# Second layer's experts from the fourth chunk on: down products as three products of halves, gate applied to each expert's sum

## The reference, cut to what matters

```python
logits = x @ router_w + router_b                      # 9 columns: 8 experts and one "null"
...                                                   # probs = softmax(logits); top 2 kept as gates
h = jax.nn.gelu(jnp.einsum('btd,edf->ebtf', x, w1), approximate=False)   # e = 8, f = 512
y = jnp.einsum('ebtf,efd->ebtd', h, w2)
out = jnp.einsum('bte,ebtd->btd', gates[..., :E], y) + gates[..., E:] * x
...
x = x + gb * out
```

## Time and profile before

| | |
|---|---|
| time, median of 3 runs | 1898.88 us |
| span of the profiled execution | 1901.1 us |
| TensorE busy | 1669.5 us, 88% of the span |
| VectorE busy | 1393.2 us, 73% |
| ScalarE busy | 790.3 us, 42% |
| GpSimd busy | 680.6 us, 36% |
| the chain that ended last, by engine | PE 34%, DVE 13%, POOL 11%, issue 10% |
| its largest line | PE psum L1428 (`down1`) 10% |
| mean granted clock of TensorE | 0.953 of full speed |
| `down1`, line 1428 | 512 records, 261.9 us busy, mean 597 ns |

### The profile page before, as it was taken

The page is one execution under the profiler, slowest core; times in us unless marked ns, Lnnn a source line. Parts: engine busy times, 40 slices in busy tenths (PEclk is TensorE's granted clock), DMA queues, the critical chain, the costliest instruction groups (busy, mean ns, idle before and its releaser), DMA issues.

```text
span 1901.1 us, 25452 instructions
## 1 busy us (share of the span) xinstructions
PE 1669.5 (88%) x7212; PEld 1043.8 (55%) x7212; DVE 1393.2 (73%) x2638; ACT 790.3 (42%) x1486; POOL 680.6 (36%) x610
## 2 busy tenths in 40 slices
PE   2789889851899999999999999999998999999999
PEld 1455555441665656656556565565665555555555
DVE  5787777558676696896987979979789678544444
ACT  1476766721433324334234253352433643433333
POOL 2011111100000492781945918639378077000000
PEclk9998989955899999999999999999999999999999
DMA  7544444010667777665666667667564111111110
GB/s 272 163 124 121 114 117 131 22 64 0 196 226 228 208 259 202 193 203 178 205 185 184 197 183 195 204 187 211 172 190 127 40 45 53 42 51 55 50 49 29
DMA packets 167960, 269.60 MB, mean 142 GB/s; under 512 B 23220, under 2 KB 61453, under 8 KB 164661
## 3 DMA queue, kind: packets, MB, share of 16 engines
q1 hardware_dynamic: 164227, 266.40, 47.5%
q10 hardware_dynamic: 1586, 1.30, 0.2%
q0 software_dynamic: 2048, 0.79, 0.2%
HBM read 233.78 MB, written 34.62 MB: 141 GB/s over the span
## 4 chain that ended last, share of the span: by engine, by line
PE 34%; DVE 13%; POOL 11%; issue 10%; DMA 3%; ACT 2%; SPq 1%; DVEq 0%; POOLq 0%; ACTq 0%
PE psum L1428 10%; POOL e_prod L1798 7%; PE psum L1321 6%; PE psum L1323 5%; PE psum L1322 5%; PE psum L1330 4%; DVE psum L1729 3%; POOL e_phi L1798 3%; DMA rw<-rw_fm 2%; DVE e_hm L1732 2%; DVE e_y L1610 2%; DVE e_vbar L1610 2%; DVE e_state L1684 1%; PE psum L1367 1%; DMA e_ring<-w_split 1%
## 5 line engine op out<-in xcount | busy, mean ns | idle before, releaser
L1553 ACT ACTIVATE e_gu<-psum 128x512 f32<-128x512 f32 (+1 forms) x368 | 219.2, 598 | 597.7 <-DVE e_hm L1732 302.4
L1321 PE MATMUL psum<-e_hhi,e_ring 128*128 128x512 f32 x704 | 432.7, 615 | 27.2 <-DMA e_ring<-w_split 9.4
L1330 PE MATMUL psum<-e_hm,w_d 128*128 128x512 f32 (+1 forms) x736 | 382.3, 601 | 15.0 <-DVE e_hm L1735 6.5
L1798 POOL TENSOR_TENSOR e_prod<-e_state,e_phi 128x512 f32<-128x512 f32 x256 | 353.8, 1420 | 2.4 <-POOL e_phi L1798 1.7
L1729 DVE TENSOR_TENSOR psum<-psum,rw 128x512 f32<-128x512 f32 x352 | 243.9, 693 | 119.7 <-PE psum L1323 87.9
L1766 DVE TENSOR_TENSOR e_hm<-psum,rw 128x512 f32<-128x512 f32 x256 | 174.6, 689 | 174.7 <-ACT psum L1578 173.6
L1322 PE MATMUL psum<-e_hhi,e_ring 128*128 128x512 f32 x704 | 279.9, 398 | 0.0
L1323 PE MATMUL psum<-e_hlo,e_ring 128*128 128x512 f32 x704 | 279.8, 397 | 0.0
L1732 DVE TENSOR_TENSOR e_hm<-psum,e_gu 128x512 f32<-128x512 f32 x352 | 243.6, 692 | 36.4 <-ACT e_gu L1553 12.5
L1428 PE MATMUL psum<-e_hm,w_gu 128*128 128x512 f32 x512 | 261.9, 597 | 6.6 <-DVE w_d L1747 5.5
L1578 ACT ACTIVATE psum<-psum 128x512 f32<-128x512 f32 x256 | 148.8, 582 | 251.6 <-PE psum L1323 233.9
(11 more groups left out here) (226 smaller groups left out, 2189.2 us busy)
## 6 DMA issues: line engine op xcount, KB each, us to landing
e_ring<-w_split SPq DMA_DIRECT2D x308, 256.0 KB, 4.0
rw<-rw_fm SPq DMA_DIRECT2D x192, 176.0 KB
qk_parts<-at_part SPq DMA_DIRECT2D x96, 192.0 KB, 2.9
rw<-gates_fm SPq DMA_DIRECT2D x72, 256.0 KB, 3.2
w_split<-e_ring SPq DMA_DIRECT2D x44, 256.0 KB, 3.2
rw<-rw_fm SPq DMA_DIRECT2D x64, 160.0 KB
at_qs<-qk_parts SPq DMA_DIRECT2D x16, 576.0 KB
at_ks<-qk_parts SPq DMA_DIRECT2D x16, 576.0 KB
```

Source lines behind the costliest of these rows:

```text
L1321: pe.matmul(out, w_hi, x_hi, start=first, stop=False)
L1330: mm = pe.matmul(ps[:, ACC, :], weights_at(T, WD + P * j, P)[0:rows(j), :], hm[0:rows(j), slot(j), :], start=(j == 0), stop=(j == HT - 1))
L1553: a(act_g[0:r, j % 2, :], ps[0:r, GB[j % 2], :], ACT.Silu).then_inc(silu_done, 1)
L1798: ins = tt(out[:, at], x[:, at], y[:, at], op)
```

## The change

The weights w2 are split too. In chunk 1, ScalarE rounds each of the 32 tiles of w2 (128x128) into the room that the first layer's down weights left (`w2_high`), and VectorE subtracts to get the low halves (`w2_low_half`, in the ring and in `sel_buf`). From chunk 3 (`HALVED`) on, Gelu goes straight from PSUM into the ring `hm`, ungated. ScalarE copies it to its high half (`gelu_high`), one tile behind the Gelu; VectorE subtracts to get its low half (`gelu_low`). `down1_halves` makes three products of halves in place of one float32 product, and sums only over the four tiles of an expert, in banks `YB` by turns. VectorE then multiplies the expert's sum by the gate and adds it to `null` (`add_expert`), at tile j = 4e + 6 for expert e, and for the last expert at tile 2 of the next chunk, followed by `add_result`, the two multiply-adds on x. `null` is now made at j = 4, and the gates' buffers come free with the expert's sum. Besides, the setup's semaphore `eps_set` is merged into `pool_done`. The core of the diff:

```diff
+            def down1_halves(c, j, k):
+                e, g = j // F1T, nth(c, j)
+                if k == HALVED:
+                    pe.wait_ge(w1l_done, T1 + j + 1)
+                    ...
+                if j % F1T == 0 and (k > HALVED or e >= 2):
+                    pe.wait_ge(gated, NE1 * (c - HALVED) + e - 1)
+                pe.wait_ge(glo_done, g + 1)
+                three(ps[:, YB[e % 2], :], part(w2_high(j)), w2_low_half(j), gelu_parts[:, 0, j % RING1, :],
+                      gelu_parts[:, 1, j % RING1, :], j % F1T == 0, j % F1T == F1T - 1).then_inc(ydown_done, 1)
...
+            def gelu_high(c, j, k):
+                ...
+                if k > HALVED or j >= RING1:
+                    act.wait_ge(ydown_done, nth(c, j) - RING1 + 1)
+                act.wait_ge(gelu_done, T1 * c + j + 1)
+                a(gelu_parts[:, 0, j % RING1, :], hm[:, j % RING1, :], ACT.Copy).then_inc(ghi_done, 1)
...
             def block1(c, k):                    # ScalarE
                 for j in range(T1):
                     g = T1 * c + j
+                    if j == 0 and k > HALVED:
+                        gelu_high(c - 1, T1 - 1, HALVED + 1)
                     if j == 0 and k > 0:
                         act.wait_ge(up1_done, g)
                         act.wait_ge(h1_kept, c + 1)
                         h_high(0, c)
                     act.wait_ge(up1_done, g + 1)
...
+                        a(hm[:, j % RING1, :], ps[:, HB[j % 2], :], ACT.Gelu).then_inc(gelu_done, 1)
+                        if j > 0:
+                            gelu_high(c, j - 1, k)
...
+                    if k == 1:
+                        if j == 0:
+                            act.wait_ge(acc_done, CHUNKS)
+                        a(part(w2_high(j)), weights_at(T, w2_low(j), P), ACT.Copy).then_inc(w1h_done, 1)
...
+            def add_expert(c, e, k):             # VectorE
+                n = NE1 * (c - HALVED) + e
+                dve.wait_ge(ydown_done, F1T * (n + 1))
+                dve.wait_ge(r1_in[e % RB_SLOTS], 16 * (NE1 // RB_SLOTS) * c + 16 * (e // RB_SLOTS + 1))
+                v.tensor_tensor(xc[:], ps[:, YB[e % 2], :], rb[:, e % RB_SLOTS, :], ALU.mult).then_inc(gated, 1)
+                dve.wait_ge(gated, n + 1)
+                v.tensor_tensor(null, null, xc[:], ALU.add).then_inc(acc1_read, 1)
...
+            def gelu_low(c, j):
+                dve.wait_ge(ghi_done, nth(c, j) + 1)
+                v.tensor_tensor(gelu_parts[:, 1, j % RING1, :], hm[:, j % RING1, :], gelu_parts[:, 0, j % RING1, :].bitcast(F32),
+                                ALU.subtract).then_inc(glo_done, 1)
...
+                    if k == 1:
+                        if j == 0:
+                            dve.wait_ge(ur_done, HT * CHUNKS)
+                        dve.wait_ge(w1h_done, T1 + j + 1)
+                        v.tensor_tensor(w2_low_half(j), weights_at(T, w2_low(j), P), part(w2_high(j)).bitcast(F32), ALU.subtract)\
+                            .then_inc(w1l_done, 1)
...
+                    if j % F1T == 2 and (k > HALVED or k == HALVED and j > F1T):
+                        e = j // F1T - 1
+                        ...
+                        add_expert(c if e >= 0 else c - 1, e % NE1, k)
+                        if e < 0:
+                            add_result(c - 1)
```

More of the change, by code:

```diff
@@ L1063, with w2_high @@
 NULL_AT = WD + P * (2 * T1 - 2 * FREE_G)
+HALVED = 3
+def w2_high(j):
+    return WD + P * j
 def experts(nc, T, A, out):
@@ L1173, in experts @@
         down1_done = sem("down1_done")
+        ghi_done = sem("ghi_done")
+        glo_done = sem("glo_done")
+        ydown_done = sem("ydown_done")
+        gated = sem("gated")
         acc1_read = sem("acc1_read")
@@ L1250, in part, with w2_low_half, nth @@
             return weights_at(T, at, P, "_r")
+        def w2_low_half(j):
+            return ring[:, P * j:P * (j + 1)] if j < T1 // 2 else T["sel_buf_r"][:, P * (j - T1 // 2):P * (j - T1 // 2 + 1)]
+        def nth(c, j):
+            return T1 * (c - HALVED) + j
         @block.sync
@@ L1455, in block1 @@
                         pass
+                    elif j >= LAG1 and k >= HALVED:
+                        down1_halves(c, j - LAG1, k)
                     elif j >= LAG1:
                         down1(c, j - LAG1, k)
+                    elif k > HALVED:
+                        down1_halves(c - 1, T1 - LAG1 + j, HALVED + 1)
                     elif k > 0:
@@ L1464, in _ @@
             for j in range(T1 - LAG1, T1):
-                down1(CHUNKS - 1, j, 1)
+                down1_halves(CHUNKS - 1, j, HALVED + 1)
         @block.scalar
@@ new lines, in add_result, with gate_tile @@
+            def add_result(c):
+                dve.wait_ge(acc1_read, HALVED + NE1 * (c - HALVED + 1))
+                for i in range(CB):
+                    b = CB * c + i
+                    x = cols(x_fm, b, SEQ)
+                    ins = v.scalar_tensor_tensor(x, null[:, i * SEQ:(i + 1) * SEQ], T["gate"][:, 3, ds(b, 1)], x, ALU.mult, ALU.add)
+                ins.then_inc(x_done, 1)
+            def gate_tile(c, j, k):
+                e, g = j // F1T, T1 * c + j
+                dve.wait_ge(gelu_done, g + 1)
+                if j % F1T == 0:
+                    dve.wait_ge(r1_in[e % RB_SLOTS], 16 * (NE1 // RB_SLOTS) * c + 16 * (e // RB_SLOTS + 1))
+                if k > 0 or j >= RING1:
+                    dve.wait_ge(down1_done, g - RING1 + 1)
+                v.tensor_tensor(hm[:, j % RING1, :], ps[:, GU1[j % 2], :], rb[:, e % RB_SLOTS, :], ALU.mult).then_inc(m_done, 1)
@@ L1761, in block1 @@
[L1761 to L1765, removed]
-                    v.tensor_tensor(hm[:, j % RING1, :], ps[:, GU1[j % 2], :], rb[:, e % RB_SLOTS, :], ALU.mult).then_inc(m_done, 1)
+                    if k >= HALVED:
+                        gelu_low(c, j)
+                    else:
+                        gate_tile(c, j, k)
@@ L1780, in _ @@
             run(dve, block0, block1)
-            result(CHUNKS - 1)
+            add_expert(CHUNKS - 1, NE1 - 1, HALVED + 1)
+            add_result(CHUNKS - 1)
         @block.gpsimd
```

42 lines of the change are left out of this document (29 added, 13 removed).

## The result

The change makes the kernel slower by 1.2%. Timed beside the kernel before, it took 1925.03 us (median of 4 runs, 1921.38 to 1926.89) against 1902.79 us (1898.11 to 1907.4), a ratio of 1.0116 with a 95% interval of 1.009 to 1.0142. The forecast was 1914 us.

What follows compares the result with a forecast made beforehand. It took TensorE, busy 88% of the span, to bound the kernel. Chunks 4 to 7 -4, clock +6, chunk 1 +10 and chunk 3 +3 gave +15 on 1898.9: 1914 us, range 1898 to 1927.

Steps and rivals of the forecast that it cites:

- The products: Down products, chunks 3 to 7: six products of halves, 1.38 us a tile in place of 1.56, 28.0 us saved.
- The sums: `add_expert` on VectorE: its two operations between two low halves make TensorE wait 0.2 us at each expert's sum.
- The chain with 0.4 of slack: Loop tile, Gelu to copy to low half: usable at G + 2.16, needed by TensorE at G + 2.56.
- The step: Between chunks: `h_low` comes last on VectorE, so `up1` to `up1` takes 5.65 us against 3.46 before.
- A loop chunk without the clock: Chunks 4 to 7: 50.35 us each against 51.32, a gain of 1.0 each, -4 us together.
- The clock: TensorE idles 3.2 us in each of four steps, then runs at half rate: 1.5 us each, +6 (bounds 0 and 6.8).
- Chunk 1: 32 subtractions of w2 on VectorE, each 0.69 us dearer beside GpSimd: chunk becomes 64.1 us, +10 (bounds 0 and 20).
- Chunk 3: First chunk with halves: 5.1 us saved, against sums, longer end and ScalarE's table loads and affine passes; net +3.
- That VectorE isn't on the path: Rival 1: products decide, neither sums nor port delay anything; -25, 1874 us, with partial effect up to 1889; chance 0.10.
- That chunk 1 hides the subtractions: Rival 2: VectorE's 12.7 us idle in chunk 1 takes them in; +5, 1904 us, no measurable change; chance 0.20.
- That the clock holds: Rival 3: no fall of the clock at the steps between chunks; +9, 1908 us; chance 0.08.
- Dearer still: Rival 4: chunk 1 near its bound of 20, chunk 3 at +5, late low halves holding up GpSimd's chain; 1926 us; chance 0.12.

Runs made afterwards that it cites:

- the second timing: The changed kernel itself timed once more, unaltered, against the kernel before: 1916.57 us (median of 6 runs), ratio 1.0085.
- both single cures: Changed kernel plus w2's high halves copied to PSUM for the subtraction, and next input's halves made ahead of the last two tiles' copies and low halves: 1893.55 us, 0.9948.
- the first experiment: Kernel before plus only the split of w2 in chunk 1, its halves unused and down products still float32: 1917.52 us, ratio 1.0088.
- the last gain: Additions moved one tile later in the kernel with halves from chunk 4, w2 split in chunk 3 and next input's halves first: 1889.9 to 1882.89 us.
- additions one tile later: Changed kernel with each addition to `null` one tile behind its multiplication, `add_result` at tile 3 instead of 2: 1909.81 us, ratio 1.0031.
- next input's halves first: Changed kernel with the next chunk's `h_high` and `h_low` made ahead of the last two tiles' copies and low halves: 1905.18 us, ratio 1.0014.

## Why the prediction was right, and where its terms were off

The sign and the two main mechanisms were right: products save what they should, and two losses, on VectorE in chunk 1 and at the step between chunks, are larger. 1925 us lies in the range, near its upper edge. In `block1` I had +15 and it is +17.5, in two executions. That this is so close is partly luck: chunks 4 to 7 without the clock came out 4 us better than forecast, chunks 1 and 3 together 6.5 us worse. Of the 11 us between 1914 and 1925, 2.5 lie in `block1`, 3.9 are the kernel before, whose median was 1902.79 beside the changed one and not 1898.88, and the other 4.7 lie ahead of `block1`. In the second timing the whole difference, 12.9 us, was below the 17.5 of `block1`, so these are scatter.

- **The products.** Six at 0.23 each: tiles follow at 1.39 where nothing waits, against my 1.38. Right.
- **The sums.** My 0.72 between multiplication and addition is 0.71. But 0.2 us for each sum was four times too much: the wait of TensorE at every fourth tile, which I had named as a sign, isn't in the trace of after, and the tiles lose 0.05. The chain with 0.4 of slack was too strict by 0.15. Tile 2 I put at 1.4; its Gelu comes 1.13 late (2.52 to 1.39). The Trainium skill ("VectorE: DVE Perf Modes", The DRAIN you can't avoid) says of a row of copies that the semaphore costs nothing extra. For these operations the two distances say otherwise, 0.62 without a wait for the one ahead and 0.71 with it.
- **The step.** 5.65 forecast, 5.48 measured, and the order in which operations follow one another is the one worked out. Putting `h_low` first returned it to 3.49.
- **A loop chunk without the clock.** 50.35 forecast, 49.31 measured; most of the difference is the sums (6 x 0.15). Chunks 4 to 7 together are 2.4 us shorter with 5.9 us of clock in them, so without the clock they came to -8 rather than -4.
- **The clock.** +6 forecast. Measured against the 49.31 of chunk 5: 2.65 in chunk 4, 0 in 5, 1.6 in 6; in chunk 7 1.6 (56.84 less 54.41 less the 0.8 behind the last `up1`): 5.9. Right in size, but not by the rule that I had from the earlier trace rows: behind one step the clock fell for 6 us, behind two for 3.4, behind one not at all. That these make four times 1.5 is luck.
- **Chunk 1.** +10 forecast, +12.8 measured, and 12.4 with the split alone. A subtraction takes 0.67 us against 0.28 undisturbed, and VectorE's busy time of 62.08 us is near the 64.1 that I worked out. The step that failed is the last: I let the idle time that stays and the lag that may grow cancel. VectorE still has 5.2 us idle, 4.8 of them waiting for Gelus, so the chunk is longer than its work.
- **Chunk 3.** +3 forecast with bounds of -1.7 and +5; it is +6.7, above my bound. I counted ScalarE's table loads and left out what they do to the clock: the low halves come late, the transposes wait 2.98 us for L730 (before, the longest wait in this chunk was 2.39 and the clock held), and TensorE runs at 0.50 for the 6 us behind that wait. What the fall costs can be read from the kernel with both single cures, whose chunk 3 is the same up to its last tiles. In its trace the transposes wait as long and the clock holds behind them (it falls later in the chunk, for 3.4 us):

```profile
1648.55 0.33 PE L737 MATMUL psum<-ident,e_nt 128*128 128x128 f32 x1 [2.99 <-DVE e_nt L730]
...
1648.00:1654.00 6.00, 4.43 (x25) 3.58 (x26) 2.48 (x6) 3.94 (x8) 0.00 (x0) 1.00 0.00 0
```

Tiles 3 to 6 of the chunk take 13.5 us there and 14.6 in the changed kernel, so this fall is worth some 1.2 of the 6.7 us; the step at the chunk's end is 2.0. The rest was not taken apart by a run. This is the term whose bounds failed.
- **The rivals.** That VectorE isn't on the path fell: TensorE waits for it at every step. That chunk 1 hides the subtractions fell with the first experiment. That the clock holds came true at one step of four. "Dearer still", 1926 us with chunk 1 near 20 and chunk 3 at +5, has the time of the first timing but not the split of it.

What stays open: what sets whether the clock falls, how the waits of chunk 3 make up its other 3.5 us, and 4 us of the last gain.

## What to carry to other kernels

An engine with much idle time can still sit on the path at the seam between two rounds: list what stands ahead of the one operation that the next round waits for, and put that operation first. It was worth 14.6 us here, with no work removed. A preparation on VectorE with both inputs in SBUF belongs where GpSimd is idle, or gets one input from PSUM: the same 32 operations cost 12 us in one chunk and 1 in another.

## What the runs showed of the hardware that I had not expected

- The clock doesn't follow from the last idle time alone. TensorE waited 3.05, 3.04, 3.12 and 3.12 us at the four steps of the changed kernel (into chunks 4 to 7); behind the first it ran at 0.50 for 6 us, behind the second at 1.00, behind the third (from 1816.70) and the fourth at 0.50 for 3.4 us:

```profile
1816.70:1820.10 3.40, 3.40 (x8) 2.72 (x9) 0.00 (x0) 0.98 (x2) 0.00 (x0) 0.50 0.09 26
1867.91:1871.31 3.40, 3.40 (x10) 2.63 (x8) 0.00 (x0) 1.56 (x3) 0.00 (x0) 0.50 0.05 19
```

In the second execution the second and the third changed places. With the additions one tile later the wait was 2.89 us at all four steps, and the clock fell behind two of them. Yet behind the shorter wait of 2.60 us at the start of chunk 1 it fell in all twelve profiled executions. Behind waits of 1.03 to 1.05 us (next input's halves first) it held at all four steps.

- Where the inputs lie decides, not the size alone: beside GpSimd 128x128 with both inputs in SBUF went from 0.28 to 0.67 us in the mean, while the gated tile of 128x512 with one input in PSUM kept its 0.68, and the 128x128 form with one input in PSUM took 0.28.
- Profiled executions reach `block1` anywhere from 1449.7 to 1460.3 us, with the same code ahead of it but for the setup's semaphore. A difference of under 5 us between two single executions says little; the chunks' lengths mostly repeat to about 0.1 us where the clock is the same.
